# State-space layers: a logarithm and its rounding rest summed on TensorE, X as first term of the output product, GpSimd drives at odd states

## Chip, cores and metric

The kernel runs on one core of one Trainium2 chip. The metric is the device time of one launch in microseconds; the profile is one profiled execution of the same program. The engines are called PE (TensorE), DVE (VectorE), ACT (ScalarE), POOL (GpSimd) and SP (SyncE, which here only issues DMAs).

## What is computed

Four layers follow one another on x of shape (4, 128, 64, 64), each as `x = x + layer(norm(x))`. Only the first two, the state-space layers, are touched. Cut to what matters:

```python
xz = seq @ W_in.T
u, z = jnp.split(xz, 2, axis=-1)
u = silu(causal_conv4(u) + conv_b)
x_dbl = u @ W_x.T
dt = jax.nn.softplus(x_dbl[..., :4] @ W_dt.T + b_dt)
Bmat, Cmat = x_dbl[..., 4:20], x_dbl[..., 20:36]
h = exp(dt * A) * h + (dt * u) * B        # per time step, 16 states
y = sum_over_states(h * C) + u * Dp
return (y * silu(z)) @ W_out.T
```

There are 256 sequences of 128 steps, 128 inner channels and 16 states. The kernel takes softplus(v) as relu(v) + log1p(e), with e = exp(-|v|), and log1p(e) as ln(1 + e) less the rounding error of 1 + e.

## The kernel before, in words

**Tiling.** `mamba_layer` treats 32 chunks of 8 sequences. A tile is 128 channels by 1024 tokens in fp32. A chunk has 16 units, one for each state s. The engines' programs are written out by hand: each engine runs the same sequence of units (`pe_unit`, `act_both`, `dve_unit`, `pool_unit`, `sp_unit`) in order and waits at semaphores. Three chunks are unrolled, then a loop takes two at a time, and the last chunk stands alone. While chunk c runs, the same units carry the preparation of chunk c+1, at the unit numbers k of the `*_prep` functions.

**A unit.** PE spreads the row of B over the partitions into `b_ps` (`pe_rows`, L441). ACT makes the decays exp(dt·A) (L533). DVE multiplies by dt·u (the drive, L563) and runs the recurrence (the scan, L577). POOL multiplies the state by the row of C (the product, L617). PE adds that product into `y_ps` (`pe_sum`, L453), three units later (`LAG`). For the five states in `POOL_UNITS`, 2, 4, 6, 8 and 10, POOL makes the drive instead, from a row that a DMA has loaded (L611), two units ahead (`DRIVE_AHEAD`); PE and DVE then have none, and ACT writes the decays into `b_ps`. There are two `b_ps` buffers, so the rows or decays of unit s wait for scan s-2. There are four state buffers, so scan s waits for the sum s-4.

**The preparation** passes its intermediate results through one PSUM buffer, `prep_ps`, in turns: transposes of x at k = 0, the convolution at 1 and 2, u (L542, DVE) at 4, the B and C rows at 5, the low part of B (L547, DVE) at 6, dt before softplus at 7, relu, |v| and exp at 8 (ACT), ln(1+e) and the rounded 1+e at 9 (L504, L506, ACT), the rounding rest `lost` at 10 (L551, DVE). The z product (PE, L430) waits for `lost`, since it overwrites `prep_ps`. The gate sigmoid takes three ACT instructions (exp, ln, exp; L510, L512, L515) at 11 and 12, and DVE multiplies by z at 13 (`sz`, L555). POOL subtracts the rest from the logarithm at 11 (L594), adds the relu part at 12 (L598) and multiplies by u at 13 (L604).

**Around the end of a chunk.** At unit 2 DVE gates y of the chunk before (`dve_gate`, L582), for which the last sum must be there. At unit 14 PE multiplies by W_out into `prep_ps` (`pe_out`, L465), after `sz`. At unit 15 DVE adds the result to X (`dve_add`, L586). SP loads the C rows one by one behind the products, writes B and C of the next chunk to DRAM at unit 11 (`C_WRITE_AT`) and loads the B rows for POOL.

The function behind the order of a DVE unit is short:

```python
def dve_unit(dve, c, par, s, prep):
    dve_drive(dve, c, par, s)
    if s == GATE_AT and not is_first(c):
        dve_gate(dve, c - 1, 1 - par)
    if prep:
        dve_prep(dve, c + 1, 1 - par, s)
    if s == ADD_AT and not is_first(c):
        dve_add(dve, c - 1)
    dve_scan(dve, c, par, s)
```

Of the kernel before, what the change touches and what calls it, by code (L numbers as in the profile page):

```python
# [16 lines left out]
P = 128  # L17
# [267 lines left out]
LOAD_AT, C_WRITE_AT = 8, 11  # L285
POOL_UNITS = (2, 4, 6, 8, 10)
# [4 lines left out]
def mamba_layer(nc, sem, tag, X, C, M, scale_c, bias_c):  # L291
# [3 lines left out]
    with Memory(nc, tag) as m:  # L295
        xs = m.sb("xs", [P, COLS])
        xt = m.sb("xt", [P, HALF])
        zero = m.sb("zero", [P, CHUNK_N])
        u = m.sb("u", [P, TOK])
# [35 lines left out]
        s_log1p = sem(f"{tag}_log1p_ready")  # L335
# [60 lines left out]
        def pe_prep(pe, n, par, k):  # L396
# [72 lines left out]

        def act_prep(act, n, par, k):  # L470
# [12 lines left out]
            if k == 4:  # L483
                wait(act, s_gu, 3 * n + 2)
                nc.scalar.activation(gu[:, :], gu[:, :], ACT.Exp, scale=-1.0).then_inc(s_gu, 1)
            if k == 5:
# [26 lines left out]
            if k == 12:  # L513
# [139 lines left out]

        def dve_unit(dve, c, par, s, prep):
# [5 lines left out]
            if s == ADD_AT and not is_first(c):  # L660
                dve_add(dve, c - 1)
# [1028 lines left out]
```

## Time and profile before

| | |
|---|---|
| median of 3 runs | 6466.08 us (6462.25 to 6472.54) |
| profiled execution, time | 6468.96 us |
| profiled execution, span | 6467.1 us |
| busy shares of the span | PE 79%, DVE 77%, ACT 51%, POOL 73% |
| mean granted PE clock | 0.919 |
| DVE scans (L577, 704 with DVE drive, 320 with POOL drive) | 1608.7 and 729.4 us |
| POOL products (L617, 1024) | 2404.3 us |
| PE sums (L453, 4096 matmul instructions) | 1987.8 us busy |

The state-space layers fill the slices 1 to 23 of the 40 in the page's second part, each slice 162 us, with the second layer's norm in between. In a timeline row the first number is the start in us from the start of the span, the second the duration; "x8" merges eight instructions in a row; the bracket is the idle time of the engine before it and what ended it. One fp32 matmul of 512 columns shows as two instructions. Ends of matmuls are modelled, so the pace of PE is read from starts.

### The profile page before, as it was taken

Reading aid. Unit: us, or ns where it says so; the run is one execution under the profiler, and the core shown is the slowest. Engines: PE = TensorE matmul, PEld = TensorE weight load, DVE = VectorE, ACT = ScalarE, POOL = GpSimd, SP = SyncE. Lnnn points to the kernel's source line nnn. Section 1 sums busy time; section 2 is a strip of 40 time slices with the busy share of each in tenths; the row PEclk is TensorE's granted clock in tenths of the full one; section 3 lists DMA queues with packets and bytes.
Section 4 is the critical chain, followed back from the end, with each engine's and each line's share of the span. In section 5 each row is a group of like instructions: output and inputs, shape, how many; then the busy total and the mean of one; then the engine's idle time right before and its main releaser. Section 6 shows DMA issues by size and latency. Waiting matters only on the chain. (4 is left out here: it accounts for less than half of the span.)

```text
span 6467.1 us, 77508 instructions
## 1 busy us (share of the span) xinstructions
PE 5083.2 (79%) x22442; PEld 2639.5 (41%) x22442; DVE 4970.1 (77%) x6243; ACT 3277.4 (51%) x3626; POOL 4744.4 (73%) x2140
## 2 busy tenths in 40 slices
PE   3888888888874888888888866852559899898980
PEld 1343333333332333333333335311336566566650
DVE  5999999999996999999999984016465665655548
ACT  3555555555543555555555530001447677677760
POOL 3999999999994999999999970000337677676760
PEclk9999999999997999999999995875879999999995
DMA  3555555555552555555555540861569999999991
GB/s 124 202 198 201 199 200 203 203 202 199 203 176 97 200 202 205 202 200 200 200 199 204 203 147 22 343 239 27 97 123 186 179 173 186 164 185 185 184 185 52
DMA packets 1414964, 1148.54 MB, mean 178 GB/s; under 512 B 1211624, under 2 KB 1216832, under 8 KB 1406656
## 3 DMA queue, kind: packets, MB, share of 16 engines
q1 hardware_dynamic: 1414850, 1147.21, 62.3%
q8 instruction: 48, 0.79, 0.0%
q14 instruction: 66, 0.54, 0.0%
HBM read 812.29 MB, written 20.68 MB: 129 GB/s over the span
## 5 line engine op out<-in xcount | busy, mean ns | idle before, releaser
L617 POOL TENSOR_TENSOR l_state<-l_state,l_c_row 128x1024 f32<-128x1024 f32 x1024 | 2404.3, 2366 | 72.6 <-DVE l_state L577 69.0
L1389 POOL TENSOR_TENSOR l3s_el<-l3s_s_sb,l3s_eh 128x1024 f16<-128x1024 f32 (+2 forms) x584 | 1168.5, 2011 | 1217.1 <-ACT l3s_s_sb L1374 1205.7
L453 PE MATMUL l_y_ps<-l_state,ident 128*128 128x512 f32 x4096 | 1987.8, 611 | 49.0 <-POOL l_state L617 48.2
L577 DVE TENSOR_TENSOR_SCAN l_state<-l_decay,l_b_ps 128x1024 f32<-128x1024 f32 x704 | 1608.7, 2285 | 74.8 <-ACT l_decay L533 3.4
L1397 DVE TENSOR_SCALAR_CACHE_REDUCE l3s_s_sb<-l3s_s_ps 128x512 f32<-128x512 f32 (+1 forms) x1096 | 753.8, 689 | 621.9 <-PE l3s_s_ps L1333 603.2
L453 PEld LDWEIGHTS l_y_ps<-l_state,ident 128*128 128x128 f32 x4096 | 781.5, 195 | 870.2 <-issue 676.6
L1346 PE MATMUL l3s_o_ps<-l3s_vt,l3s_et 128*128 128x257 f16 x4368 | 879.5, 279 | 191.0 <-DMA l3s_et<-l3s_el 125.1
L1373 ACT ACTIVATE l3s_eh<-l3s_s_sb,l3s_shift 128x1024 f16<-128x1024 f32 (+2 forms) x584 | 634.5, 1087 | 535.4 <-DMA l3s_et<-l3s_el 423.0
L563 DVE TENSOR_TENSOR l_b_ps<-l_dtu,l_b_ps 128x1024 f32<-128x1024 f32 x704 | 850.4, 1208 | 30.2 <-PE l_b_ps L441 28.4
L441 PE MATMUL l_b_ps<-l_bc,mamba_pick 128*128 128x512 f32 x1408 | 575.1, 491 | 295.5 <-DVE l_state L577 285.6
L1348 PE MATMUL l3s_o_ps<-l3s_vt,l3s_et 128*128 128x129 f16 x4368 | 788.6, 224 | 0.0
L611 POOL TENSOR_TENSOR l_b_row<-l_b_row,l_dtu 128x1024 f32<-128x1024 f32 x320 | 756.2, 2363 | 0.2
L577 DVE TENSOR_TENSOR_SCAN l_state<-l_b_ps,l_b_row 128x1024 f32<-128x1024 f32 x320 | 729.4, 2279 | 5.1 <-POOL l_b_row L611 3.2
L1374 ACT ACTIVATE l3s_s_sb<-l3s_s_sb,l3s_shift 128x1024 f32<-128x1024 f32 (+2 forms) x584 | 629.8, 1078 | 0.0
L1346 PEld LDWEIGHTS l3s_o_ps<-l3s_vt,l3s_et 128*128 128x128 f16 x4368 | 435.0, 100 | 436.4 <-issue 204.6
L441 PEld LDWEIGHTS l_b_ps<-l_bc,mamba_pick 128*128 128x128 f32 x1408 | 230.6, 198 | 761.3 <-DVE l_state L577 583.8
L1331 PE MATMUL l3s_s_ps<-l3s_xh 128*128 128x512 f16 (+1 forms) x1096 | 426.9, 389 | 91.1 <-DVE l3s_xl L1310 69.4
L1348 PEld LDWEIGHTS l3s_o_ps<-l3s_vt,l3s_et 128*128 128x128 f16 x4368 | 435.3, 100 | 111.3 <-issue 6.6
L533 ACT ACTIVATE l_decay<-l_dt,l0m_A 128x1016 f32<-128x1016 f32 x352 | 393.0, 1134 | 141.2 <-POOL l_dt L598 99.1
L533 ACT ACTIVATE l_decay<-l_dt,l1m_A 128x1016 f32<-128x1016 f32 x352 | 393.0, 1134 | 140.4 <-POOL l_dt L598 99.6
L1332 PE MATMUL l3s_s_ps<-l3s_xl,l3s_xh 128*128 128x512 f16 (+1 forms) x1096 | 426.1, 389 | 0.0
L1333 PE MATMUL l3s_s_ps<-l3s_xh,l3s_xl 128*128 128x512 f16 (+1 forms) x1096 | 425.2, 388 | 0.0
(335 smaller groups left out, 5428.1 us busy)
## 6 DMA issues: line engine op xcount, KB each, us to landing
l_c_row<-l_c_rows SPq DMA_DIRECT2D x1024, 512.0 KB, 3.9
l_b_row<-l_c_rows SPq DMA_DIRECT2D x320, 512.0 KB, 4.9
l_ring_a<-in_L_conv_W SPq DMA_DIRECT2D x28, 1024.0 KB, 11.1
l2b_ring_b<-in_L_conv_W SPq DMA_DIRECT2D x26, 1024.0 KB, 11.3
l_xs<-X SPq DMA_DIRECT2D x64, 256.0 KB, 5.3
l_ring_a<-in_L_conv_W SPq DMA_DIRECT2D x14, 704.0 KB, 12.7
l2b_ring_b<-in_L_conv_W SPq DMA_DIRECT2D x13, 704.0 KB, 12.7
l_ring_a<-in_L_conv_W SPq DMA_DIRECT2D x14, 640.0 KB, 12.1
```

What stands on the lines that cost most here:

```text
L441: last = nc.tensor.matmul(b_ps[s % PAIRS][:, half(h)], C["pick"][:, s * P:(s + 1) * P], bc[:, par, half(h)], start=True, stop=True)
L453: last = nc.tensor.matmul(y_ps[:, half(h)], C["ident"][:, :], state[:, s % STATES, half(h)], start=False, stop=(s == S - 1))
L533: nc.scalar.activation(seq(to), seq(dt[:, par, :]), ACT.Exp, scale=M["A"][:, s:s + 1]).then_inc(s_decay, 1)
L563: nc.vector.tensor_tensor(b_ps[s % PAIRS][:, :], dtu[:, par, :], b_ps[s % PAIRS][:, :], ALU.mult).then_inc(s_drive, 1)
L577: nc.vector.tensor_tensor_scan(state[:, s % STATES, :], by, add, 0.0, ALU.mult, ALU.add).then_inc(s_scan, 1)
L611: nc.gpsimd.tensor_tensor(row, row, dtu[:, par, :], ALU.mult).then_inc(s_bdrive, 1)
L617: nc.gpsimd.tensor_tensor(state[:, s % STATES, :], state[:, s % STATES, :], c_row[:, s % C_ROWS, :], ALU.mult).then_inc(s_hc, 1)
L1346: high = lambda stop: nc.tensor.matmul(o_ps[par][:, 0:2 * P + 1], et[:, 0, slot, j, :], vt[:, mt, 0:2 * P + 1], start=(mt == 0), stop=stop)
L1348: lows = lambda: nc.tensor.matmul(o_ps[par][:, P:2 * P + 1], et[:, 1, slot, j, :], vt[:, mt, P:2 * P + 1], start=False, stop=False)
L1373: nc.scalar.activation(eh[:, part, off:off + EXPW], src, ACT.Exp, bias=shift[:, par:par + 1]).then_inc(s_eh, 1)
L1389: nc.gpsimd.tensor_tensor(el[:, part, off:off + EXPW], s_sb[:, par, j * EXPW:(j + 1) * EXPW], eh[:, part, off:off + EXPW], ALU.subtract).t ...
L1397: nc.vector.tensor_scalar(s_sb[:, par, kb * W:(kb + 1) * W], s_ps[(par * NB + kb) % SLOTS][:, 0:W], 0.0, None, ALU.add, ALU.max, accum_out ...
```

## The change

The sum ln(1+e) plus the rest moves from POOL to PE: two matmuls with the identity for each half, at k = 11, write `ln_e + gu` into `prep_ps`, and ACT copies it back to `gu` (k = 11). For that `gu` holds the rest with the other sign (ACT's L519 makes -1 - e, DVE's L568 adds 1 and e). The z product goes from k = 10 to 12 and waits for the copy; the three ACT instructions of the z sigmoid all stand at 12. POOL loses L594. X becomes the first term of the output product, and an ACT copy (`act_store`) takes the place of DVE's add. POOL's drives go to the states 3, 5, 7, 9 and 11. The third ACT instruction of the u sigmoid moves from k = 4 to 3, `c_out` shares memory with `gz` (with a wait for the write to DRAM ahead of the z sigmoid), and that write goes from unit 11 to 10.

```diff
-LOAD_AT, C_WRITE_AT = 8, 11
-POOL_UNITS = (2, 4, 6, 8, 10)
+LOAD_AT, C_WRITE_AT = 8, 10
+POOL_UNITS = (3, 5, 7, 9, 11)
...
-        c_out = m.sb("c_out", [P, TOK])
+        c_out = gz
...
-            if k == 10:
+            if k == 11:
                 wait(pe, s_lost, n + 1)
+                wait(pe, s_ln, n + 1)
+                for h in range(2):
+                    nc.tensor.matmul(prep_ps[:, half(h)], C["ident"][:, :], ln_e[:, half(h)], start=True, stop=False)
+                    last = nc.tensor.matmul(prep_ps[:, half(h)], C["ident"][:, :], gu[:, half(h)], start=False, stop=True)
+                last.then_inc(s_log1p, 1)
+            if k == 12:
+                wait(pe, s_exact, n + 1)
                 for h in range(2):
                     nc.tensor.matmul(prep_ps[:, half(h)], M["w_z"][rows(h), :], xt[rows(h), :],
...
+            nc.tensor.matmul(prep_ps[:, 0:COLS], C["ident"][:, :], X[:, bass.ds(c * COLS, COLS)], start=True, stop=False)
             for n in range(CHUNK_N):
...
-                                        M["w_out"][:, :], start=True, stop=True)
+                                        M["w_out"][:, :], start=False, stop=(n == CHUNK_N - 1))
...
             if k == 11:
+                wait(act, s_log1p, n + 1)
+                nc.scalar.activation(gu[:, :], prep_ps[:, :], ACT.Copy).then_inc(s_exact, 1)
+            if k == 12:
+                wait(act, s_cw, 16 * (n + 1))
                 wait(act, s_pz, 2 * n + 2)
                 wait(act, s_sz, n)
                 nc.scalar.activation(gz[:, :], prep_ps[:, :], ACT.Exp, scale=-1.0).then_inc(s_gz, 1)
                 wait(act, s_gz, 3 * n + 1)
                 nc.scalar.activation(gz[:, :], gz[:, :], ACT.Ln, bias=1.0).then_inc(s_gz, 1)
-            if k == 12:
                 wait(act, s_gz, 3 * n + 2)
                 nc.scalar.activation(gz[:, :], gz[:, :], ACT.Exp, scale=-1.0).then_inc(s_gz, 1)
...
-                nc.vector.scalar_tensor_tensor(gu[:, :], gu[:, :], -1.0, prep_ps[:, :],
-                                               ALU.add, ALU.subtract).then_inc(s_lost, 1)
+                nc.vector.scalar_tensor_tensor(gu[:, :], gu[:, :], 1.0, prep_ps[:, :],
+                                               ALU.add, ALU.add).then_inc(s_lost, 1)
...
-        def dve_add(dve, c):
...
+        def act_store(act, c):
+            wait(act, s_out, c + 1)
+            nc.scalar.activation(X[:, bass.ds(c * COLS, COLS)], prep_ps[:, 0:COLS], ACT.Copy).then_inc(s_x, 1)
...
-            if k == 11:
-                wait(pool, s_ln, n + 1)
-                wait(pool, s_lost, n + 1)
-                nc.gpsimd.tensor_tensor(ln_e[:, :], ln_e[:, :], gu[:, :], ALU.subtract).then_inc(s_log1p, 1)
             if k == 12:
-                wait(pool, s_log1p, n + 1)
+                wait(pool, s_exact, n + 1)
...
-                nc.gpsimd.tensor_tensor(dt[:, par, :], ln_e[:, :], dt[:, par, :], ALU.add).then_inc(s_dt, 1)
+                nc.gpsimd.tensor_tensor(dt[:, par, :], gu[:, :], dt[:, par, :], ALU.add).then_inc(s_dt, 1)
```

How the instructions stand now. PE, before, from the sum of state 6 at unit 9 to the sum of state 9 at unit 12 (`hc_ready` is a POOL product, `state_ready` a scan):

```order
L453 MATMUL l0_y_ps<-l0_state,ident 128x512 [waits l0_hc_ready]
L453 MATMUL l0_y_ps<-l0_state,ident 128x512
L453 MATMUL l0_y_ps<-l0_state,ident 128x512 [waits l0_hc_ready]
L453 MATMUL l0_y_ps<-l0_state,ident 128x512
L430 MATMUL l0_prep_ps<-l0_xt,l0m_w_z 128x512 [waits l0_lost_ready]
L430 MATMUL l0_prep_ps<-l0_xt,l0m_w_z 128x512
L441 MATMUL l0_b_ps1<-l0_bc,mamba_pick 128x512 [waits l0_state_ready]
L441 MATMUL l0_b_ps1<-l0_bc,mamba_pick 128x512
L453 MATMUL l0_y_ps<-l0_state,ident 128x512 [waits l0_hc_ready]
L453 MATMUL l0_y_ps<-l0_state,ident 128x512
```

PE, with the change, the same engine from the sum of state 8 at unit 11 to the rows of state 13:

```order
L462 MATMUL l0_y_ps<-l0_state,ident 128x512 [waits l0_hc_ready]
L462 MATMUL l0_y_ps<-l0_state,ident 128x512
L433 MATMUL l0_prep_ps<-l0_ln_e,ident 128x512 [waits l0_ln_ready,l0_lost_ready]
L434 MATMUL l0_prep_ps<-l0_gu,ident 128x512
L433 MATMUL l0_prep_ps<-l0_ln_e,ident 128x512
L434 MATMUL l0_prep_ps<-l0_gu,ident 128x512
L450 MATMUL l0_b_ps0<-l0_bc,mamba_pick 128x512 [waits l0_state_ready]
L450 MATMUL l0_b_ps0<-l0_bc,mamba_pick 128x512
L462 MATMUL l0_y_ps<-l0_state,ident 128x512 [waits l0_hc_ready]
L462 MATMUL l0_y_ps<-l0_state,ident 128x512
L439 MATMUL l0_prep_ps<-l0_xt,l0m_w_z 128x512 [waits l0_log1p_read_out]
L450 MATMUL l0_b_ps1<-l0_bc,mamba_pick 128x512 [waits l0_state_ready]
```

What now follows the wait for `lost` is four matmuls instead of two, one sum later, and the z product stands behind the read-out and another sum. DVE, with the change, from the drive of state 10 to the scan of state 13:

```order
L580 TENSOR_TENSOR l0_b_ps0<-l0_dtu,l0_b_ps0 128x1024 [waits l0_b_row]
L568 SCALAR_TENSOR_TENSOR l0_gu<-l0_gu,l0_prep_ps 128x1024 [waits l0_one_plus_e]
L594 SCALAR_TENSOR_TENSOR l0_state<-l0_decay,l0_b_ps0 128x1024 [waits l0_drive_ready,l0_y_summed,l0_decay_ready]
L594 SCALAR_TENSOR_TENSOR l0_state<-l0_b_ps1,l0_b_row 128x1024 [waits l0_start_cleared,l0_pool_drive_ready,l0_y_summed,l0_decay_ready]
L580 TENSOR_TENSOR l0_b_ps0<-l0_dtu,l0_b_ps0 128x1024 [waits l0_b_row]
L594 SCALAR_TENSOR_TENSOR l0_state<-l0_decay,l0_b_ps0 128x1024 [waits l0_drive_ready,l0_y_summed,l0_decay_ready]
L580 TENSOR_TENSOR l0_b_ps1<-l0_dtu,l0_b_ps1 128x1024 [waits l0_b_row]
L572 TENSOR_TENSOR l0_sz<-l0_prep_ps,l0_gz 128x1024 [waits l0_sigmoid_z]
L594 SCALAR_TENSOR_TENSOR l0_state<-l0_decay,l0_b_ps1 128x1024 [waits l0_drive_ready,l0_y_summed,l0_decay_ready]
```

Before, `lost` was followed by one scan and the drive of state 11; now by two scans and the drive of state 12, and it stands between a drive and its scan.

## Rows read from the trace of the kernel before

**Rows 1.** Page, part 2: busy tenths of DVE and POOL in 40 equal slices.

```profile
DVE  5999999999996999999999984016465665655548
POOL 3999999999994999999999970000337677676760
```

**Rows 2.** Timeline, DVE: the `lost` instruction of the second and last preparation, both layers.

```profile
151.21 1.20 DVE L551 SCALAR_TENSOR_TENSOR l_gu<-l_gu,l_prep_ps 128x1024 f32<-128x1024 f32 x1
...
1852.59 1.20 DVE L551 SCALAR_TENSOR_TENSOR l_gu<-l_gu,l_prep_ps 128x1024 f32<-128x1024 f32 x1
...
2069.48 1.20 DVE L551 SCALAR_TENSOR_TENSOR l_gu<-l_gu,l_prep_ps 128x1024 f32<-128x1024 f32 x1
...
3771.40 1.20 DVE L551 SCALAR_TENSOR_TENSOR l_gu<-l_gu,l_prep_ps 128x1024 f32<-128x1024 f32 x1
```

**Rows 3.** Timeline, DVE: units 14 and 15 of one chunk.

```profile
1076.54 1.21 DVE L563 TENSOR_TENSOR l_b_ps<-l_dtu,l_b_ps 128x1024 f32<-128x1024 f32 x1
1077.88 2.29 DVE L577 TENSOR_TENSOR_SCAN l_state<-l_decay,l_b_ps 128x1024 f32<-128x1024 f32 x1
1080.09 1.21 DVE L563 TENSOR_TENSOR l_b_ps<-l_dtu,l_b_ps 128x1024 f32<-128x1024 f32 x1
1081.20 0.68 DVE L586 TENSOR_TENSOR X<-X,l_prep_ps 128x512 f32 x1
1081.80 2.28 DVE L577 TENSOR_TENSOR_SCAN l_state<-l_decay,l_b_ps 128x1024 f32<-128x1024 f32 x1
```

**Rows 4.** Timeline, DVE: scan of state 2 and drive of state 11, next chunk.

```profile
1092.13 2.28 DVE L577 TENSOR_TENSOR_SCAN l_state<-l_b_ps,l_b_row 128x1024 f32<-128x1024 f32 x1
...
1120.94 1.21 DVE L563 TENSOR_TENSOR l_b_ps<-l_dtu,l_b_ps 128x1024 f32<-128x1024 f32 x1
```

**Rows 5.** Timeline, POOL: first and eleventh instruction of an unbroken stretch.

```profile
1084.29 2.36 POOL L617 TENSOR_TENSOR l_state<-l_state,l_c_row 128x1024 f32<-128x1024 f32 x1 [0.80 <-DVE l_state L577]
...
1107.45 2.38 POOL L611 TENSOR_TENSOR l_b_row<-l_b_row,l_dtu 128x1024 f32<-128x1024 f32 x1
```

**Rows 6.** Timeline, PE at full granted clock: sums, rows, z product.

```profile
1094.51 3.60 PE L453 MATMUL l_y_ps<-l_state,ident 128*128 128x512 f32 x8
1098.01 0.73 PE L441 MATMUL l_b_ps<-l_bc,mamba_pick 128*128 128x512 f32 x2
1098.58 1.88 PE L453 MATMUL l_y_ps<-l_state,ident 128*128 128x512 f32 x4
...
1118.87 1.13 PE L430 MATMUL l_prep_ps<-l_xt,l0m_w_z 64*128 64x512 f32 x4 [2.38 <-DVE l_gu L551]
```

**Rows 7.** Timeline, PE around `lost` of the chunk before, then a window with granted clock.

```profile
1055.59 0.73 PE L441 MATMUL l_b_ps<-l_bc,mamba_pick 128*128 128x512 f32 x2 [1.23 <-DVE l_state L577]
1056.15 3.87 PE L453 MATMUL l_y_ps<-l_state,ident 128*128 128x512 f32 x8
1062.42 1.39 PE L430 MATMUL l_prep_ps<-l_xt,l0m_w_z 64*128 64x512 f32 x4 [2.40 <-DVE l_gu L551]
1064.76 2.78 PE L453 MATMUL l_y_ps<-l_state,ident 128*128 128x512 f32 x4
```

**Rows 8.** Windows: PE, PEld, DVE, ACT, POOL busy, PEclk, DMA share, GB/s.

```profile
1063.00:1066.00 3.00, 3.00 (x8) 1.50 (x5) 2.57 (x2) 2.09 (x3) 3.00 (x2) 0.53 0.57 184
```

**Rows 9.** Timeline, ACT: z sigmoid (exp, ln) and a decay.

```profile
1120.08 1.03 ACT L510 ACTIVATE l_gz<-l_prep_ps 128x1024 f32<-128x1024 f32 x1 [2.06 <-PE l_prep_ps L430]
1121.13 1.06 ACT L512 ACTIVATE l_gz<-l_gz 128x1024 f32<-128x1024 f32 x1
1122.10 1.13 ACT L533 ACTIVATE l_decay<-l_dt,l0m_A 128x1016 f32<-128x1016 f32 x1
```

**Rows 10.** Timeline: end of the first preparation of layer 0, before the first unit.

```profile
109.77 1.22 DVE L551 SCALAR_TENSOR_TENSOR l_gu<-l_gu,l_prep_ps 128x1024 f32<-128x1024 f32 x1 [8.91 <-ACT l_gu L506]
111.04 2.08 PE L430 MATMUL l_prep_ps<-l_xt,l0m_w_z 64*128 64x512 f32 x4 [6.59 <-DVE l_gu L551]
...
118.39 1.23 DVE L563 TENSOR_TENSOR l_b_ps<-l_dtu,l_b_ps 128x1024 f32<-128x1024 f32 x1 [0.74 <-POOL l_dtu L604]
```

More of the change, by code:

```diff
@@ L298, in mamba_layer @@
         zero = m.sb("zero", [P, CHUNK_N])
+        minus_one = m.sb("minus_one", [P, 1])
         u = m.sb("u", [P, TOK])
@@ L334, in mamba_layer @@
         s_lost = sem(f"{tag}_lost_ready")
-        s_log1p = sem(f"{tag}_log1p_ready")
+        s_log1p = sem(f"{tag}_log1p_summed")
+        s_exact = sem(f"{tag}_log1p_read_out")
         s_dt = sem(f"{tag}_dt_ready")
@@ L477, in act_prep @@
                 wait(act, s_pu, 2 * n + 2)
-                wait(act, s_log1p, n)
+                wait(act, s_dt, n)
                 nc.scalar.activation(gu[:, :], prep_ps[:, :], ACT.Exp, scale=-1.0,
@@ L482, in act_prep @@
                 nc.scalar.activation(gu[:, :], gu[:, :], ACT.Ln, bias=1.0).then_inc(s_gu, 1)
-            if k == 4:
                 wait(act, s_gu, 3 * n + 2)
@@ L490, in act_prep @@
                 wait(act, s_cw, 16 * n)
+                wait(act, s_sz, n)
                 nc.scalar.activation(c_out[C_AT:C_AT + BLOCK, :], prep_ps[C_AT:C_AT + BLOCK, :],
@@ L503, in act_prep @@
                 wait(act, s_abs, 2 * n + 2)
+                wait(act, s_log1p, n)
                 nc.scalar.activation(ln_e[:, :], prep_ps[:, :], ACT.Ln, bias=1.0).then_inc(s_ln, 1)
                 wait(act, s_u, n + 1)
-                nc.scalar.activation(gu[:, :], prep_ps[:, :], ACT.Identity, bias=1.0).then_inc(s_one, 1)
+                if is_first(n):
+                    wait(act, s_edge, 2)
+                nc.scalar.activation(gu[:, :], prep_ps[:, :], ACT.Identity, scale=-1.0,
+                                     bias=minus_one[:, 0:1]).then_inc(s_one, 1)
             if k == 11:
+                wait(act, s_log1p, n + 1)
+                nc.scalar.activation(gu[:, :], prep_ps[:, :], ACT.Copy).then_inc(s_exact, 1)
+            if k == 12:
+                wait(act, s_cw, 16 * (n + 1))
                 wait(act, s_pz, 2 * n + 2)
@@ L582, in dve_gate @@
             nc.vector.tensor_tensor(yz[:, :], sz[:, par, :], y_ps[:, :], ALU.mult).then_inc(s_yz, 1)
-        def dve_add(dve, c):
-            wait(dve, s_out, c + 1)
-            nc.vector.tensor_tensor(X[:, bass.ds(c * COLS, COLS)], X[:, bass.ds(c * COLS, COLS)], prep_ps[:, 0:COLS],
-                                    ALU.add).then_inc(s_x, 1)
+        def act_store(act, c):
+            wait(act, s_out, c + 1)
+            nc.scalar.activation(X[:, bass.ds(c * COLS, COLS)], prep_ps[:, 0:COLS], ACT.Copy).then_inc(s_x, 1)
         def pool_prep(pool, n, par, k):
-            if k == 11:
-                wait(pool, s_ln, n + 1)
-                wait(pool, s_lost, n + 1)
-                nc.gpsimd.tensor_tensor(ln_e[:, :], ln_e[:, :], gu[:, :], ALU.subtract).then_inc(s_log1p, 1)
             if k == 12:
-                wait(pool, s_log1p, n + 1)
+                wait(pool, s_exact, n + 1)
                 wait(pool, s_pos, n + 1)
-                nc.gpsimd.tensor_tensor(dt[:, par, :], ln_e[:, :], dt[:, par, :], ALU.add).then_inc(s_dt, 1)
+                nc.gpsimd.tensor_tensor(dt[:, par, :], gu[:, :], dt[:, par, :], ALU.add).then_inc(s_dt, 1)
             if k == 13:
@@ L652, in act_both @@
                 act_prep(act, c + 1, 1 - par, s)
+            if s == ADD_AT and not is_first(c):
+                act_store(act, c - 1)
         def dve_unit(dve, c, par, s, prep):
@@ L659, in dve_unit @@
                 dve_prep(dve, c + 1, 1 - par, s)
-            if s == ADD_AT and not is_first(c):
-                dve_add(dve, c - 1)
             dve_scan(dve, c, par, s)
@@ L718, in _ @@
                 run(act, act_both)
+                act_store(act, LAST)
             @block.vector
@@ L725, in _ @@
                 dve_gate(dve, LAST, LAST % 2)
-                dve_add(dve, LAST)
             @block.gpsimd
@@ L731, in _ @@
                 nc.gpsimd.memset(zero[:, :], 0.0).then_inc(s_edge, 1)
+                nc.gpsimd.memset(minus_one[:, :], -1.0).then_inc(s_edge, 1)
                 for slot in range(DECAYS):
```

## The prediction

> **What bounds the kernel now.** I read first the forty slices of the page: through both state-space layers DVE and POOL are busy nine tenths and more of every slice [rows 1]. Two engines are full at once, so taking work from one is worth only what the other allows. Next the pace of the chunks, from the starts of `lost` (L551), which comes once in each: 30 periods in layer 0 take 1852.59 - 151.21 = 1701.38 us and 30 in layer 1 take 1701.92 us, 56.72 us a chunk [rows 2].
>
> How much of that is DVE's own pace? Starts in its timeline give the price of each instruction to the next: a scan 2.21 us, a drive whose scan follows at once 1.34 us (the scan waits for its result), a drive with another instruction in between 1.11 us, the addition to X 0.60 us [rows 3]. From the scan of state 2 to the drive of state 11 there are 28.81 us without a marked wait [rows 4]. The rest of the chunk, from that drive to the next scan of state 2, is 7 scans, 5 bare drives (11, 12, 14, 0, 1), 2 drives with something between, `sz`, the gate (1.11 each) and the addition: 15.5 + 6.7 + 2.2 + 2.2 + 0.6 = 27.2. Together 56.0, so 0.7 us of a chunk is waiting. POOL's pace is (1107.45 - 1084.29)/10 = 2.32 us an instruction [rows 5]. A chunk has 16 products, 5 drives and 3 of the preparation, 24 instructions, 55.6 us. PE is in neither place first, but its order decides when the others get their inputs.
>
> **The change, without waits.** POOL loses one instruction: 23 x 2.32 = 53.3 us. DVE loses the addition, 0.60. Its drives are now at 0, 1, 2, 4, 6, 8, 10 and 12 to 15, and gate, u, B's low part and `lost` fall between a drive and its scan. Three fewer drives are bare (6 instead of 9), 3 x 0.23 = 0.7. DVE's own pace becomes 56.0 - 0.6 - 0.7 = 54.7 us. If nothing else ended last, a chunk would take 2.0 us less. The question is whether DVE's inputs come in time.
>
> **A walk from the end of scan 2 (time 0) to `sz`.** POOL waits for scan 2: behind scan 0 it has two products and one drive, 6.95 us, while DVE needs 1.34 + 2.21 + 1.11 + 1.11 + 2.21 = 7.98. From 0 POOL is unbroken: products 2, 3, 4, 5, 6, 7, 8 and the drives 5, 7, 9, ten instructions, so product 8 is there at 23.2. DVE reaches the drive of state 12 after exactly the instructions of [rows 4] (9 scans, 4 drives, u, the low part, `lost`), with three drives no longer bare: 28.81 - 0.7 = 28.1. `lost` is done by 28.1 - 4.4 = 23.7, two scans earlier.
>
> PE, in order: sum of state 8, rest of the logarithm, rows of 12, sum of 9, z product, rows of 13. Four matmul instructions of a sum start 3.60 - 1.88 = 1.72 apart, rows 0.57, a z product about 1.06 [rows 6]. Sum 8 can start at 23.25 and takes 1.8 with its first load, so the four new matmuls (eight instructions, 3.44) run from 25.1 to 28.5 although `lost` was ready at 23.7. The rows of 12 are ready 0.73 later, 29.2. The drive of 12 therefore waits 1.2 us. ACT copies the sum out from 28.7, then writes the decay of 12 behind it: 28.7 + 1.0 + 1.13 = 30.8 [rows 9] (the copy is taken as long as the first activation there). The scan of 12 starts at 30.8 instead of 28.1 + 1.34 = 29.4: **first wait, 1.4 us**.
>
> The z product follows the sum of 9 (29.1 to 30.8) and is done near 31.9. The copy, done at 29.7, is hidden behind that sum. Three dependent activations at 1.05 apart [rows 9] end at 32.0 + 2.1 + 1.05 = 35.15. DVE has the scan of 12 from 30.8, the drive of 13 from 33.0 and wants `sz` at 34.1: **second wait, 1.05 us**. Before, the z product stood at unit 10 and had three units of room.
>
> So a chunk takes 54.7 + 1.4 + 1.05 = 57.15 us at full granted clock, 0.4 more than 56.72.
>
> **PE's clock.** Before, PE waits 2.4 us for `lost`; in one chunk z then takes 1.39 us and a sum 2.78 instead of 1.88, with a granted clock of 0.53 in that window, half speed being 1.2 GHz; after the same idle time in the next chunk z took 1.13 [rows 6 to 8]. An idle time of 1.23 us alone was followed by full speed [rows 7]. With the change that long wait is gone, but by the walk two shorter ones stand close together ahead of the sum of 7 (waits for scan 8 and for product 7, about 1.2 and 1.0 us). I take a third of the chunks to fall to half, between none and all. A fall there delays the sums of 7 and 8 by about 1.2 us (a sum at half clock costs 0.9 to 1.7 more), straight into the first wait: 0.4 us a chunk on average. The forecast is 57.55 us, 0.83 more, times 60: **+50 us**.
>
> The Trainium skill (TensorE: Matmul & The Clock Gate, Part 1) says that the gate throttles by default and that sustained work releases it; by that rule alone the added matmuls should keep PE at full clock, and the sum would be 26 us instead of 50. The trace agrees only in part: it shows half clock in an engine that is busy most of the time.
>
> **Ends of the layers.** Before the first unit nothing covers the preparation. There `lost` starts at 109.77 and the first drive at 118.39, and z ran at half clock, 2.08 instead of 1.13 [rows 10, 6]. Now: eight matmul instructions (3.6 at full, 7 at half clock), copy 1.0, then z, sigmoid and `sz` (2.1 + 3.2 + 1.2), against 7.4 us from the end of `lost` to the drive: 11.1 to 14.5, so 4 to 7 more; the POOL steps run beside. I take 6. X's matmul at the end of the last chunk adds 0.9, the copy costs what the addition did. Two layers: **+14 us**.
>
> **What costs nothing.** The matmul of X (0.86) stands in unit 14 behind the sum of 11; the rows of 15 behind it are wanted 2 us later. ACT's store waits there for the output product, with decay 15 already written. The u sigmoid ends 3 us before u is wanted. The write of C and B on SP goes one unit earlier, behind the load of a C row, and product 6, which releases that row, is seven POOL instructions from time 0, 16.2 us; the z sigmoid that now waits for the write starts at 32, so it has 15 us of room. POOL's drives of 9 and 11 are ready 0.7 and 0.3 us before their scans; if that cover went, each would cost what POOL is late.
>
> **Sum.** 6468.96 + 50 + 14 = 6533 for the profiled execution; the median of the runs lies 3 lower, so **6530 us**. The forecast's own range is a chunk between 57.0 and 58.1: 6497 to 6563.
>
> **Rivals.**
> 1. *The waits do not appear and DVE's own pace rules.* This needs PE to have the logarithm summed 1.4 us earlier than I walk it, and `gz` 1 us earlier. For it: both engines lose work and PE waits 2.4 us at that place now. Against: sum 8 stands ahead and hangs on POOL's unbroken chain. Price: 54.9 x 60 instead of 56.72 x 60 is -109, ends +14: about 6371. Chance 0.12.
> 2. *Only one wait stays.* For example, product 8 comes a little earlier and the drive of 12 is met; then 54.7 + 1.1 to 1.4 is 56.0, -43 + 14: 6437; with some half-clock chunks it comes back to 6466. Chance 0.09, of which 0.07 within 0.2% of before.
> 3. *Half clock under the new matmuls in nearly every chunk.* Then the 3.44 us too stretch by up to 1.7: 58.3 to 58.9, +95 to +131, ends +14: 6575 to 6611. For: half clock now follows in most chunks whose z product waits. Against: less idle time. Chance 0.12.
> 4. *Full clock throughout.* PE loses its one long idle time and no chunk falls to half: 57.15 us, 60 x 0.43 = +26, ends +14: 6506. For: 1.23 us idle left the clock alone. Against: two gaps in a row. Chance 0.20. This is what the page on TensorE named above would give.
>
> The forecast has 0.47. A measurement of this kernel can tell 0.2%, 13 us, from no change. Faster: rival 1 and a part of 2, 0.14. Within 0.2%: 0.07. Slower: 0.79. The range runs from 6455, leaving rival 1 outside, to 6590, leaving the upper half of rival 3 outside.
>
> **What would show it.** DVE should show waits before the drive or scan of state 12 (on L450 rows or on L550's decay) of 1 to 2.5 us and before `sz` (on L532) near 1 us in nearly every chunk; starts of `lost` 57.1 to 58 us apart; POOL idle 3 to 4 us a chunk instead of 1; no addition on DVE. The forecast is wrong if `lost` comes every 55 us, if `sz` finds its sigmoid ready, or if sum 8 starts well ahead of `lost`.

## The result, and the profile after

The changed kernel takes 6566.39 us (median of 4 runs, 6561.65 to 6568.84), the kernel before in the same comparison 6464.16: ratio 1.0154, 95% interval 1.0139 to 1.0169. It is slower by 102 us, where 64 were forecast. The profiled execution took 6568.84, its span is 6566.6, 99.5 more than before.

**Pace of the chunks.** The timeline of the changed kernel, DVE, `lost` of the second and last preparation of both layers, as in [rows 2]:

```profile
158.97 1.21 DVE L568 SCALAR_TENSOR_TENSOR l_gu<-l_gu,l_prep_ps 128x1024 f32<-128x1024 f32 x1
1900.93 1.21 DVE L568 SCALAR_TENSOR_TENSOR l_gu<-l_gu,l_prep_ps 128x1024 f32<-128x1024 f32 x1
2128.60 1.21 DVE L568 SCALAR_TENSOR_TENSOR l_gu<-l_gu,l_prep_ps 128x1024 f32<-128x1024 f32 x1
3870.41 1.21 DVE L568 SCALAR_TENSOR_TENSOR l_gu<-l_gu,l_prep_ps 128x1024 f32<-128x1024 f32 x1
```

The 60 periods take 1741.96 + 1741.81 us, 58.06 each instead of 56.72: +80.5 us of the 99.5. The other 19.0 lie outside these periods.

**What DVE waits for.** The waits of the changed kernel from 400 to 1800 us, some 25 chunks (us in total, times, longest). For DVE this is the whole list:

```profile
POOL l_state L629 <- DVE l_state L594: 108.5, 112, 1.3
DVE l_b_ps L580 <- PE l_b_ps L450: 47.1, 25, 2.3
DVE l_sz L572 <- ACT l_gz L532: 26.7, 25, 1.1
DVE l_state L594 <- ACT l_decay L550: 9.8, 25, 0.4
```

Before, the drives waited 11.5 us for rows in the same stretch and `sz` never. Now three waits stand in every chunk, together 3.3 us, and POOL, freed of an instruction, is 4.5 us a chunk idle for scans (0.9 before). The costliest groups of the page for the whole span say the same of the product and the drive (in the kernel before they had 72.6 and 30.2 us of idle time ahead of them):

```profile
L629 POOL TENSOR_TENSOR l_state<-l_state,l_c_row 128x1024 f32<-128x1024 f32 x1024 | 2407.3, 2367 | 300.1 <-DVE l_state L594 300.1
L580 DVE TENSOR_TENSOR l_b_ps<-l_dtu,l_b_ps 128x1024 f32<-128x1024 f32 x704 | 850.9, 1209 | 125.3 <-PE l_b_ps L450 125.3
```

**A chunk at full granted clock.** Timeline of PE, then of DVE:

```profile
679.52 0.74 PE L450 MATMUL l_b_ps<-l_bc,mamba_pick 128*128 128x512 f32 x2 [0.95 <-DVE l_state L594]
681.23 1.98 PE L462 MATMUL l_y_ps<-l_state,ident 128*128 128x512 f32 x4 [0.97 <-POOL l_state L629]
683.55 1.98 PE L462 MATMUL l_y_ps<-l_state,ident 128*128 128x512 f32 x4 [0.34 <-POOL l_state L629]
685.37 1.02 PE L433 MATMUL l_prep_ps<-l_ln_e,ident 128*128 128x512 f32 x2
...
688.41 1.03 PE L450 MATMUL l_b_ps<-l_bc,mamba_pick 128*128 128x512 f32 x2
```

```profile
689.47 1.23 DVE L580 TENSOR_TENSOR l_b_ps<-l_dtu,l_b_ps 128x1024 f32<-128x1024 f32 x1 [1.20 <-PE l_b_ps L450]
691.09 2.29 DVE L594 TENSOR_TENSOR_SCAN l_state<-l_decay,l_b_ps 128x1024 f32<-128x1024 f32 x1 [0.39 <-ACT l_decay L550]
...
695.57 1.22 DVE L572 TENSOR_TENSOR l_sz<-l_prep_ps,l_gz 128x1024 f32<-128x1024 f32 x1 [1.06 <-ACT l_gz L532]
```

This is the walk of the prediction: sum 8 waits for POOL, then the logarithm (3.04 us from start to start up to the rows of 12), then the drive.

**A chunk with half clock.** PE, DVE and ACT of an earlier chunk, and PE's windows (columns as in [rows 8]):

```profile
562.75 0.73 PE L450 MATMUL l_b_ps<-l_bc,mamba_pick 128*128 128x512 f32 x2 [0.95 <-DVE l_state L594]
564.46 5.40 PE L462 MATMUL l_y_ps<-l_state,ident 128*128 128x512 f32 x8 [0.97 <-POOL l_state L629]
569.69 1.02 PE L433 MATMUL l_prep_ps<-l_ln_e,ident 128*128 128x512 f32 x2
...
572.73 1.02 PE L450 MATMUL l_b_ps<-l_bc,mamba_pick 128*128 128x512 f32 x2
573.59 1.88 PE L462 MATMUL l_y_ps<-l_state,ident 128*128 128x512 f32 x4
575.40 1.13 PE L439 MATMUL l_prep_ps<-l_xt,l0m_w_z 64*128 64x512 f32 x4
```

```profile
565.91 1.21 DVE L568 SCALAR_TENSOR_TENSOR l_gu<-l_gu,l_prep_ps 128x1024 f32<-128x1024 f32 x1
...
573.79 1.23 DVE L580 TENSOR_TENSOR l_b_ps<-l_dtu,l_b_ps 128x1024 f32<-128x1024 f32 x1 [2.29 <-PE l_b_ps L450]
```

```profile
573.33 1.02 ACT L523 ACTIVATE l_gu<-l_prep_ps 128x1024 f32<-128x1024 f32 x1 [7.21 <-PE l_prep_ps L434]
574.25 1.13 ACT L550 ACTIVATE l_decay<-l_dt,l0m_A 128x1016 f32<-128x1016 f32 x1
576.65 1.02 ACT L528 ACTIVATE l_gz<-l_prep_ps 128x1024 f32<-128x1024 f32 x1 [1.27 <-issue]
```

```profile
564.00:566.00 2.00, 1.54 (x2) 0.65 (x3) 2.00 (x3) 1.25 (x3) 2.00 (x2) 0.67 0.28 107
566.00:568.00 2.00, 2.00 (x4) 0.83 (x3) 2.00 (x2) 0.12 (x1) 2.00 (x2) 0.50 0.49 190
568.00:570.00 2.00, 2.00 (x6) 0.93 (x5) 2.00 (x2) 0.00 (x0) 2.00 (x2) 0.97 0.58 238
```

The same two idle times, 0.95 and 0.97, but here a granted clock of 0.50, 1.2 GHz, follows for some 3 us. The matmuls of the logarithm start 1.1 us later after the rows of state 10 (6.94 us instead of 5.85) and the wait at the drive is 2.29 instead of 1.20; `lost` was ready 2.6 us before the matmuls that use it. In the profiled execution 40 of the 60 periods are of this kind (58.3 to 58.5 us) and 20 of the other (57.3 to 57.4).

**The first preparation**, on several engines:

```profile
112.03 1.22 DVE L568 SCALAR_TENSOR_TENSOR l_gu<-l_gu,l_prep_ps 128x1024 f32<-128x1024 f32 x1 [9.30 <-ACT l_gu L519]
113.31 2.08 PE L433 MATMUL l_prep_ps<-l_ln_e,ident 128*128 128x512 f32 x2 [6.68 <-DVE l_gu L568]
...
119.14 1.02 ACT L523 ACTIVATE l_gu<-l_prep_ps 128x1024 f32<-128x1024 f32 x1 [7.13 <-PE l_prep_ps L434]
120.21 1.13 PE L439 MATMUL l_prep_ps<-l_xt,l0m_w_z 64*128 64x512 f32 x4 [1.11 <-ACT l_gu L523]
...
124.71 1.22 DVE L572 TENSOR_TENSOR l_sz<-l_prep_ps,l_gz 128x1024 f32<-128x1024 f32 x1 [11.45 <-ACT l_gz L532]
125.85 1.22 DVE L580 TENSOR_TENSOR l_b_ps<-l_dtu,l_b_ps 128x1024 f32<-128x1024 f32 x1
```

From the end of `lost` to the first drive 12.6 us, where [rows 10] have 7.4.

### The profile page after: what moved, and what is told of

Read it like the earlier page. It is cut to its first block and busy times, and to the rows that moved or that the text cites. A ratio compares the mean times of both kernels' runs of the same rounds, so it can differ in the third digit from the quotient of the medians.

```text
span 6566.6 us, 79116 instructions
## 1 busy us (share of the span) xinstructions
PE 5358.6 (82%) x23082; PEld 2744.5 (42%) x23082; DVE 4917.9 (75%) x6179; ACT 3392.3 (52%) x3754; POOL 4603.1 (70%) x2078
## 5 line engine op out<-in xcount | busy, mean ns | idle before, releaser
L594 DVE TENSOR_TENSOR_SCAN l_state<-l_decay,l_b_ps 128x1024 f32<-128x1024 f32 x704 | 1607.7, 2284 | 66.7 <-ACT l_decay L550 24.3
L594 DVE TENSOR_TENSOR_SCAN l_state<-l_b_ps,l_b_row 128x1024 f32<-128x1024 f32 x320 | 724.6, 2264 | 3.0 <-POOL l_b_row L623 3.0
```

The lines of the kernel that those rows point to most:

```text
L594: nc.vector.tensor_tensor_scan(state[:, s % STATES, :], by, add, 0.0, ALU.mult, ALU.add).then_inc(s_scan, 1)
```

## The experiments

Each starts from the changed kernel unless it says otherwise. The table has the changed kernel and the ten that start from it: DVE's own pace (period less its marked waits), its waits at the drive of 12, the scan of 12 and `sz`, all of a chunk at full clock; how many of the 60 periods are the long kind with half clock (their length); the time; the ratio to the kernel before with its 95% interval. e1_even and e2_half_sum are single runs and have no ratio.

| run | own | drive 12 / scan 12 / `sz` | period | long ones | us | ratio |
|---|---|---|---|---|---|---|
| the change | 54.69 | 1.20 / 0.40 / 1.06 | 57.34 | 40 (58.4) | 6566 | 1.0154 [1.0139, 1.0169] |
| e1_even | 55.63 | 0.50 / 0.39 / 1.06 | 57.58 | 18 (59.3) | 6561 | |
| e2_half_sum | 54.92 | 0 / 0 / 1.43 | 56.35 | 13 (56.8) | 6455 | |
| e3_z_first | 54.75 | 1.20 / 0.40 / 0 | 56.34 | 14 (57.4) | 6471 | 1.0005 [0.9995, 1.0014] |
| e5_rows_thrice | 54.69 | 1.22 / 0.39 / 1.06 | 57.37 | 0 | 6517 | 1.0071 [1.0055, 1.0088] |
| e6_drive5_early | 54.69 | 1.01 / 0.40 / 1.06 | 57.16 | 50 (58.25) | 6560 | 1.0138 [1.0121, 1.0155] |
| e7_decay_first | 54.83 | 1.20 / 0 / 1.32 | 57.34 | 40 (58.4) | 6562 | 1.0142 [1.0125, 1.0159] |
| e8_all | 54.83 | 1.00 / 0 / 0.33 | 56.17 | 37 (57.2) | 6490 | 1.0032 [1.0019, 1.0044] |
| e9_z_thrice | 54.75 | 1.22 / 0.40 / 0 | 56.37 | 0 | 6455 | 0.9979 [0.9969, 0.9988] |
| e10_z_decay_thrice | 54.82 | 1.23 / 0 / 0.33 | 56.38 | 0 | 6455 | 0.9978 [0.9968, 0.9987] |
| e11_all_thrice | 54.82 | 1.04 / 0 / 0.33 | 56.19 | 0 | 6443 | 0.9962 [0.9948, 0.9976] |

The two runs that start from the kernel before, e4_store_only and e12_store_thrice, stand at the end.

**1. GpSimd's drives at even states again.**

```diff
-POOL_UNITS = (3, 5, 7, 9, 11)
+POOL_UNITS = (2, 4, 6, 8, 10)
```

> The changed kernel with POOL's drives back at the even states 2, 4, 6, 8, 10. My reading (PE's queue behind lost sets the first wait): the drive that needs PE's rows is then state 11, one scan (2.2 us) after lost instead of two, and the four bare drives come back (DVE's own pace 54.7 + 0.7 = 55.4). By the same walk the wait before a drive grows from 1.2 or 2.3 to 4 to 5 us, the wait before sz disappears, and the period is 59.4 to 60.5 us against 58.05: 6640 to 6710 us. Rival: the odd states themselves cost the time (they put gate, u and lost between a drive and its scan and bring POOL's drives closer to their scans); then this kernel is faster than the changed one, 6470 to 6520.

6561.18 us: 79 below the expected range, and not the rival's time either. The place of the matmuls in PE's order is not that of the expectation: within a unit the rows come first, so drive 11 stood ahead of the four matmuls and only drive 12 behind them. What this run does show is the worth of the odd states: own pace 55.63 instead of 54.69, so they save 0.94 (four drives fewer are bare, four times 0.23), but the wait at the drive of 12 grows from 0.50 to 1.20 with them. Net 0.23 us a chunk at full clock, and over all 60 periods a mean of 58.11 against 58.06: nothing.

**2. Half of the sum.** The two matmuls that add the rounding rest are left out.

```diff
-nc.tensor.matmul(prep_ps[:, half(h)], C["ident"][:, :], ln_e[:, half(h)], start=True, stop=False)
-last = nc.tensor.matmul(prep_ps[:, half(h)], C["ident"][:, :], gu[:, half(h)], start=False, stop=True)
+last = nc.tensor.matmul(prep_ps[:, half(h)], C["ident"][:, :], ln_e[:, half(h)], start=True, stop=True)
```

> The changed kernel with two of the four new matmuls left out: the rounding rest is not added to the logarithm, the rest of the computation stands. My reading: 1.72 us less between lost and the rows of state 12, so the drive of 12 waits 0 (full clock) or about 0.6 (half clock under the sums before), the wait before sz stays near 0.7, period 55.5 to 56.0: about 6430 to 6455 us. Rival (the z product's late place alone costs the time, and the drive waits for something else such as POOL): only sz matters, the period falls by less than 0.5 us, over 6530 us.

6454.51 us, at the upper end of the range, but the period is 56.4 on average where 55.5 to 56.0 was expected. With 1.7 us less of matmuls the waits at drive and scan of 12 are gone at full clock; `sz` takes 1.43, twice the 0.7 expected, since DVE now comes to it earlier. So the first wait, 1.60 us, goes when the inserted matmuls are 1.7 us shorter, and the sigmoid's chain is a second limit close behind. An order with the four matmuls ahead of the sum of 8, which `lost` would have allowed, was not run: how much of the first wait is their place and how much their length is not separated.

**3. The z product first.** z product and rows of 13 go ahead of the sum of 9.

```diff
+            if prep and s == 12:
+                pe_prep(pe, c + 1, 1 - par, s)
+                return
+            if prep and s == 13:
+                pe_sum(pe, c, par, s - 1 - LAG)
```

> The changed kernel with PE's order changed at units 12 and 13: z product and the rows of state 13 ahead of the sum of state 9. My reading: z starts when the copy is done, about 1 us earlier, so the 1.06 us before sz goes to 0 to 0.1; the first wait stays (1.2 or 2.3, and 0.4 before the scan). Period 57.0, 62 x 1.06 = 65 us less: about 6500. Rival: ACT's three activations behind the decay of 12 set sz, not the place of z in PE; then sz waits as long as now and the time stays at 6566. A second rival: the idle time of PE while it waits for the copy brings the half clock there, which gives back some 20 us.

6471.23 us (10 runs), the kernel before 6469.06. DVE's waits from 400 to 1800 us in this kernel:

```profile
DVE l_b_ps L580 <- PE l_b_ps L450: 34.9, 24, 2.3
DVE l_state L594 <- ACT l_decay L550: 9.4, 24, 0.4
```

The wait at `sz` is gone (1.0 x 60 = 60 us), as expected, and, not foreseen, the half clock is rarer: 14 periods instead of 40, worth 26 x 1.1 = 29 us: 89 of the 95. So the time is 29 us below the 6500 expected.

**4. Does the idle time bring the half clock?** The rows of state 10, which stand between the two idle times, are written three times over.

```diff
-            for h in range(2):
+            for again in range(3 if s == 10 else 1):
+                for h in range(2):
```

> The changed kernel with PE writing the rows of state 10 three times over (same values), which fills 1.15 us of the idle time between that and the sum of state 7; DVE wants these rows 1.5 us after the first are ready, so nothing is delayed. My reading: 20 of 30 chunks lose 1.1 us because PE fell to half clock after idling 0.95 and 0.97 us on both sides of these rows; with the second gap filled nearly all chunks show the 1.2 us wait, the period is 57.35 to 57.6 and the time about 6525 to 6540. Rival: the 2.3 us waits come from something else (POOL, a DMA) with the half clock as by-product; then the waits stay and the time is 6566 or a little more.

6517.02 us, 49 less than the changed kernel. PE's timeline at the place in question:

```profile
557.88 1.67 PE L451 MATMUL l_b_ps<-l_bc,mamba_pick 128*128 128x512 f32 x6 [0.95 <-DVE l_state L595]
559.61 1.98 PE L463 MATMUL l_y_ps<-l_state,ident 128*128 128x512 f32 x4
561.92 1.98 PE L463 MATMUL l_y_ps<-l_state,ident 128*128 128x512 f32 x4 [0.33 <-POOL l_state L630]
```

(Lines behind the edit are one higher.) The second idle time is filled, all 60 periods are 57.4, and the waits of a period are those of the full-clock chunk to 0.03 us. So the half clock costs the changed kernel 60 x 0.69 = 41 us in the periods, and some 4 more behind the last `lost` of the two layers together. The rest of the 49 cannot be put down to it: the layers behind the second one, which no edit here touches, took 2597 to 2611 us in the 14 profiled executions, 6 less here than with the change. The time lies 8 us below the expected range.

**5. Two small edits by themselves.** First GpSimd's drive of state 5 at unit 2 instead of 3:

```diff
-            if s + DRIVE_AHEAD in POOL_UNITS:
-                pool_drive(pool, c, par, s + DRIVE_AHEAD)
+            for k in POOL_UNITS:
+                if s == (2 if k == 5 else k - DRIVE_AHEAD):
+                    pool_drive(pool, c, par, k)
```

> The changed kernel with POOL's drive of state 5 issued at unit 2 instead of 3, into POOL's idle time ahead of product 2. My reading (POOL's unbroken chain from product 2 to product 8 sets when sum 8 and the four matmuls run): product 8 comes 0.95 us earlier, the drive of 12 waits 0.25 instead of 1.2; the gap in PE ahead of the sum of 7 closes, so half clock becomes rarer. Period 56.4 to 57.0 against 58.05: 6470 to 6505. Rival: lost, not product 8, starts the four matmuls; then nothing moves and the time stays at 6566.

6560.0 us: missed. POOL's timeline shows where the gain stopped:

```profile
599.61 2.36 POOL L623 TENSOR_TENSOR l_b_row<-l_b_row,l_dtu 128x1024 f32<-128x1024 f32 x1
601.93 4.67 POOL L629 TENSOR_TENSOR l_state<-l_state,l_c_row 128x1024 f32<-128x1024 f32 x2
607.23 2.36 POOL L629 TENSOR_TENSOR l_state<-l_state,l_c_row 128x1024 f32<-128x1024 f32 x1 [0.64 <-DVE l_state L594]
```

The drive fills POOL's wait for scan 2, but then the product of 4 has to wait for scan 4, and the unbroken chain to product 8 starts there: 0.2 us are won, where the expectation counted on 0.95. Nor did the gap ahead of the sum of 7 close: it is 0.79 us, and 50 periods in place of 40 fell to half clock, so that the mean, 58.05, is that of the changed kernel.

Then ACT's decay of 12 ahead of the copy of the logarithm, and nothing else:

```diff
-            act_unit(act, c, par, s)
+            if s != 12 or not prep:
+                act_unit(act, c, par, s)
+            if prep and s == 11:
+                act_unit(act, c, par, 12)
```

> The changed kernel with ACT's decay of state 12 ahead of the read-out copy instead of behind it. My reading: the 0.4 us wait of scan 12 goes, but sz still comes when the z sigmoid is done, so the wait before sz grows from 1.06 to about 1.45 and the time stays within 5 us of 6566. Rival (the waits add up independently): 0.4 x 60 = 24 us less, 6542.

6562.48 us, as expected: the 0.40 at the scan of 12 moves to `sz` (1.06 to 1.32, and 0.14 of own pace).

**6. All three together**, z first, the early drive, the decay first.

> The changed kernel with all three edits: z product and rows of 13 ahead of sum 9, drive of state 5 at unit 2, decay of 12 ahead of the copy. My reading: each wait of the walk loses its cause, 0.2 us is left at the drive of 12, period 54.9 to 55.3: 6375 to 6405 us, faster than before by 1 to 1.5%. Rival: removing one wait uncovers another (POOL's drives of 9 and 11, the gate, the copy that PE waits for with half clock behind it); then the period is 55.7 or more and the time 6430 or more.

6489.54 us: 85 above the expected range, slower than the z product alone, and in the rival's range. Two steps failed. A full-clock period is 56.17, down 1.17 from the change but some 1.0 above the 54.9 to 55.3 expected (about 64 us): 1.00 us is left at the drive of 12 where 0.2 was expected, since the early drive is worth only 0.2, and 0.33 comes back at `sz`. And 37 periods are long by 1.07 us (40 us), although nothing was put down for the clock. It is the second alone that makes this kernel slower than e3_z_first, whose full-clock period is 56.34.

**7. The same with the clock held.** The repeated rows of experiment 4 on top of 3, of 3 with the decay first, and of 6.

> The changed kernel with the z product and the rows of state 13 ahead of the sum of state 9 (as in the run e3_z_first, 6471) and with the rows of state 10 written three times over (as in e5_rows_thrice). In e3_z_first 47 chunks took 56.34 us and 13, those with a half granted clock after the two idle gaps of PE, 57.4. Theory (gaps bring the half clock, and repeated matmuls between them keep the clock up, whatever stands at the z product): all 60 chunks take 56.34, 14 us less than e3_z_first, 6450 to 6462. Rival (e5_rows_thrice had its full clock for another reason, such as the point of time at which z stands): some 6471, with periods of 57.4 left.

6454.82 us: confirmed, no long period. (The trace of e3_z_first has 46 periods of 56.3 and 14 of 57.4, not 47 and 13.)

> The same, and the decay of state 12 ahead of ACT's copy of the logarithm. Theory: the wait for that decay (0.40 us a chunk at scan 12) goes; alone it had come back at sz, where the z product now has time. DVE's own pace rises by 0.14 as in e7_decay_first, so 0.26 us a chunk less than e9_z_thrice, 16 us if nothing shows at sz, 4 us less than e9 if the 0.33 seen at sz in e8_all stands here too: 6438 to 6455. This might be below the kernel before (6464 to 6470). Rival (the first wait grows by what the second gives back): the same as e9_z_thrice within 3 us.

6455.27 us: the rival's time, by another way. The first wait does not grow; that at the scan goes, and 0.33 come at `sz` and 0.07 in own pace. With both orders a chunk is 56.37 or 56.38 us, so it is the chain from product 8 through sum, logarithm, copy, z product and sigmoid that sets it, not any one wait on it.

> e8_all (z product first, GpSimd's drive of state 5 two units earlier, decay of state 12 first; 6490) with the rows of state 10 three times over. In e8_all 23 chunks took 56.17 us and 37, with the half clock, 57.2. Theory (the early drive gained 0.2 us of wait and lost it to a half clock that came more often): with the gaps filled all take 56.17, 60 x 0.64 = 38 us less, 6445 to 6460. Rival (GpSimd's early drive costs by itself, at the next product, whatever the clock): it stays above 6475.

6442.94 us: confirmed, 56.19 on average (56.07 to 56.22), 47 less than e8_all, against 38 expected; the periods give 39. Against e10_z_decay_thrice, from which it differs by the early drive alone, a period is 0.20 shorter and the time 12 us less. So the early drive's 0.2 us, which starts that chain sooner, is real; in e6_drive5_early and e8_all the clock had hidden it.

**8. X in the output product by itself.** The kernel before, with the matmul of X and ACT's store in place of DVE's addition, nothing else:

```diff
+            nc.tensor.matmul(prep_ps[:, 0:COLS], C["ident"][:, :], X[:, bass.ds(c * COLS, COLS)], start=True, stop=False)
...
-                dve_add(dve, c - 1)
+                act_store(act, c - 1)
```

> The kernel before with one part of the change alone: X as first term of the output product and ACT's store in place of DVE's addition. My reading: 0.60 us of DVE a chunk goes (own pace 56.0 to 55.4), PE's extra 0.86 us costs nothing; POOL at 24 instructions, 55.6 us, then holds DVE back and keeps part of it: 0.2 to 0.6 us a chunk, so 12 to 36 us less than before, about 6445. Rival: the extra matmul delays the rows of state 15 or the transposes behind it; then a wait appears on L441's counterpart at unit 15 and the time is that of before or more.

6433.98 us, ratio 0.9947, 95% interval 0.9930 to 0.9964: faster than both kernels, at the upper end of the expected gain. Its parts are others than expected. DVE's own pace is 55.67 and not 55.4, because the addition had stood between the drive of 15 and its scan: that drive is now bare and costs 1.34 instead of 1.11, so the addition by itself is worth 0.37 and not 0.60. And POOL keeps nothing of it: the marked waits fell too, from 0.74 to 0.52 us a chunk. In most of layer 0 the periods alternate between 55.84 and 56.78; the mean of the 60 is 56.19. Behind the idle 2.4 us ahead of the z product, which this kernel still has, the clock falls in both kinds. In the long ones it has fallen when the z product starts (its four instructions start over 1.02 us instead of 0.54), in the short ones it falls about 1.2 us later, and DVE waits 0.17 us for its rows instead of 1.12.

**9. And the clock held there too**, by repeating the rows of state 9.

> The kernel before with X as first term of the output product and ACT's store (as in e4_store_only, 6434), and with the rows of state 9, which stand between PE's idle 1.23 us and its idle 2.37 us around the z product, written three times over. In e4_store_only the periods alternate between 55.84 and 56.78 us, the longer with a half clock after that idle time and 1.12 us of waiting at the drive of state 11 in the place of 0.17. Theory (filled gaps keep the clock up): nearly all chunks take 55.84, 60 x 0.47 = 28 us less, 6400 to 6415. The copies end at about 600.5 of that trace, the drive of state 9 starts at 600.67, so they hold nothing up. Rival (1.15 us more of work in 3.6 idle us is too little here): 6430 to 6437, periods as they are.

6413.32 us, ratio 0.9908, 95% interval 0.9892 to 0.9925: the fastest kernel of the study. PE where the z product waits, now 1.74 us instead of 2.4, in one chunk:

```profile
540.50 3.60 PE L454 MATMUL l_y_ps<-l_state,ident 128*128 128x512 f32 x8
545.83 1.13 PE L430 MATMUL l_prep_ps<-l_xt,l0m_w_z 64*128 64x512 f32 x4 [1.74 <-DVE l_gu L553]
```

The time is in the expected range, but not for the expected 55.84 in nearly all periods. DVE's wait for rows is gone, and 47 periods take 55.5 to 55.8 us, 2 take 56.0. In the other 11, at 57.2 to 57.4, the next limit shows. DVE's waits from 400 to 1800 us, the whole list, and a window with the busy time of all engines (columns as in [rows 8]):

```profile
DVE l_yz L584 <- PE l_y_ps L454: 6.5, 4, 1.8
```

```profile
400.00:1700.00 1300.00, 1155.28 (x3360) 530.85 (x3359) 1262.45 (x745) 741.88 (x838) 1295.29 (x560) 0.99 0.60 204
```

POOL is busy 1295 of 1300 us; 24 instructions at 2.32 us are 55.6, the short period. In the long period that begins at 655.90, PE had waited 1.24 us for POOL's product of 13, ran at a clock of 0.50 behind that, and the gate found its last sum 1.58 us late. In this kernel half clock is rarer, not gone.

## Why the prediction was right, and where its size was off

- **The whole:** the forecast was 6530, with a band of its own from 6497 to 6563; the median is 6566, in the range of the prediction but 3 us above that band. The mechanism and the three terms (walk, clock, ends) are the ones that the trace shows. All three were put too low, the clock by most: 24 us instead of 43.
- **DVE's own pace, 54.7:** 54.69. The addition at 0.60 and three bare drives fewer at 0.23 were sized rightly together. By parts it is 0.37 for the addition (e4_store_only, which makes the drive of 15 bare) and 0.94 for the odd states (e1_even).
- **The walk at full clock, waits 1.4 and 1.05, period 57.15:** 1.20 + 0.40, 1.06, and 57.34 (20 periods of the change; 57.37 in the 60 of e5_rows_thrice). That sum 8 stands ahead of the logarithm and hangs on POOL's chain is shown by the rows (sum 8 waits 0.34 us for POOL's product while `lost` is long done) and by e11_all_thrice against e10_z_decay_thrice (an earlier start of POOL's chain takes 0.20 off every period). e2_half_sum shows that shorter matmuls remove the first wait, and e10_z_decay_thrice that a swap inside the chain moves nothing. 60 x 0.62 = +37 us of the result.
- **Half clock in a third of the chunks, 1.2 us each, +0.4 on average:** this is the step that was mis-sized. The price was near, 1.08 us; the share was two thirds. 40 x 1.08 = +43 us, where 24 were put down (60 x 0.4). The rows of before had 1.23 us idle with full speed behind it [rows 7], and no two such idle times close together; the third, between none and all, was a guess from nothing nearer. Even for its one long idle time the trace of before tells more than the two chunks that were read: the z product ran at half clock in 21 of 60 chunks, and within 3 us the clock fell in 43. e5_rows_thrice shows that the idle time is needed: work put into the second of the two removed every long period. It does not show why 40 chunks fall and 20 do not.
- **Full clock throughout (rival 4, 6506):** e5_rows_thrice, the change with nothing but the clock held, took 6517, so that rival was priced well and its condition was not met. The rule of the Trainium skill (TensorE: Matmul & The Clock Gate, Part 1), that sustained work releases the throttle, would have put the changed kernel there if an engine that is busy most of the time counts as one with sustained work. The trace does not bear that reading out: PE is busy in 1193.83 of the 1300 us from 400 to 1700, and still falls to half clock in two chunks of three.
- **Ends of the layers, +14:** +21, and 19 outside the periods in all. From the first `lost` to the second it takes 5.5 and 5.3 us more in the two layers, for which 6 were taken (5.2 of it before the first drive of layer 0, 12.6 against 7.4). From the last `lost` to the last store of X it takes 5.2 and 4.8 more, for which only 0.9, the matmul of X, was put down. The missing term is waiting: the last chunk with a preparation has its waits at drive, scan and `sz` behind its `lost`, outside the 60 periods, and the chunk behind it waits at its drive of state 4, which before it never did:

```profile
1941.65 1.23 DVE L580 TENSOR_TENSOR l_b_ps<-l_dtu,l_b_ps 128x1024 f32<-128x1024 f32 x1 [2.65 <-PE l_b_ps L450]
```

  The rest reads as scatter, not as an effect of the change. `lost` of the first preparation starts 2.3 us later (112.03 against 109.77), but in e12_store_thrice, whose code up to there is that of the kernel before, it starts at 111.89. The layers behind the second one are 4.3 us shorter than in the kernel before; no edit touches them.
- **Rival 1, the waits do not appear,** and **rival 2, only one wait stays:** not so, all three stand in every chunk. **Rival 3, half clock under the new matmuls in nearly every chunk:** they run at full clock in all 60 periods (3.03 us from the first to the rows of 12); the half clock lies under the sums ahead of them, as forecast. **What costs nothing:** no wait in DVE's list names the store, the u sigmoid, the write of C and B or POOL's drives.
- **Two parts that might have been forecast as gains:** X in the output product is one, -0.5% alone (experiment 8). Odd states gain nothing within this change, since what DVE saves it waits for at the drive of 12 (experiment 1); on the kernel before they were not run by themselves. What made the kernel slower is the logarithm's matmuls and the z product where they stand in PE's order. With that order repaired and the clock held (e11_all_thrice, 6443) it is still slower than X alone with the clock held (e12_store_thrice, 6413).

The account between the two spans: +37.2 (walk) + 43.2 (clock) + 20.9 (ends) + 2.3 and - 4.1 (scatter outside) = 99.5.

## What to carry to other kernels

An instruction taken from a full engine can be worth nothing if what replaces it stands, on the engine that takes it over, behind a result of the first one: here POOL saved 2.32 us a chunk and waited for scans instead, because the logarithm was put behind the sum that POOL's product of state 8 releases. Ask of each moved step what is ahead of it in its new queue, and what starts that; where several waits lie on one chain, only its start or its length is worth an edit. And where PE falls to half clock behind gaps of a microsecond, compare two variants with the clock held as well (by repeated matmuls in the gap that write the same values) before calling one edit better: the early drive looked worthless in e6_drive5_early and in e8_all, and was worth 12 us with the clock held.

## What the runs showed that was not expected

- Two idle times of PE of 0.95 and 0.97 us with 0.73 us of work between them were followed by a granted clock of 0.50 for about 3 us in 40 of 60 chunks, and by full clock in the rest, in rows whose two idle times read alike (0.93 to 0.96 and 0.96 to 1.00 us in both kinds). With 1.13 and 0.79 us around the rows (e8_all) it was 37, with nearly the same in e6_drive5_early 50. In e3_z_first, with 0.94 and 0.97, only 14: that kernel differs behind this place, not at it, so something further off decides too. The order is no accident: in most of the change one or two long periods follow each short one, in e6_drive5_early four, in e4_store_only the kinds alternate. What decides stays open.
- Filling such a gap with matmuls that compute nothing new made four kernels faster: 6566 to 6517, 6471 to 6455, 6490 to 6443 and 6434 to 6413 us. They take 1.15 us of PE a chunk.
- The matmuls of the logarithm, whose inputs are ready, ran at full clock in all 60 periods, although in 40 of them sums 7 and 8 right before them ran at half.
